# ScalarE's order in the attention with k's high part last, and a normalising stage written out batch by batch, on one core

## The reference

```
x = x + attention(layernorm(x))
x = x + ffn(layernorm(x))            # top 128 of 1024 rows go through gelu(x W1 + b1) W2
attention, for each head h and batch b:
    q, k, v = rope(x Wq), rope(x Wk), x Wv;  g = sigmoid(x Wg)    # three gates for each row and head
    p_cmp = softmax over the means of 64 keys;  p_slc = softmax(q k^T), causal;  p_swa = softmax(q k^T) in a window of 64
    o = g_cmp p_cmp v_cmp + g_slc p_slc v + g_swa p_swa v
out = o Wo
```

## Time and profile before

| | |
|---|---|
| Median of 3 runs | 2583.2 us (2579.54 to 2590.18) |
| The profiled execution | 2591.42 us, its span 2589.3 us |
| Mean granted TensorE clock | 0.978 |
| TensorE busy | 2455.9 us, 95% of the span |
| VectorE / ScalarE / GpSimd busy | 1858.3 / 1412.3 / 1602.1 us |
| Normalising | from 0 to about 100 us of the span |
| Attention | from about 100 to 1970 us |
| Projection with Wo and feed-forward | from 1970 us to the end |

### The profile page before, as it was taken

One profiled execution on the slowest core, in us unless ns is written; L12 is line 12 of the kernel. 1 busy time (PEld: TensorE's weight loads), 2 busy tenths in 40 slices (PEclk: granted clock), 3 DMA queues, 4 the chain that ended last, 5 costly groups with the idle time before them and its releaser, 6 DMA issues. The chain is left out here.

```text
span 2589.3 us, 48591 instructions
## 1 busy us (share of the span) xinstructions
PE 2455.9 (95%) x12944; PEld 2085.2 (81%) x12944; DVE 1858.3 (72%) x5923; ACT 1412.3 (55%) x3810; POOL 1602.1 (62%) x1177
## 2 busy tenths in 40 slices
PE   4799999999999999999999999999996999999998
PEld 3688888888888888888888888888885888887776
DVE  6377878887787878787887878778883576676223
ACT  6466666666666666566666666666663222223342
POOL 0367777777777778677777777777762443443342
PEclk8899999999999999999999999999998999999999
DMA  3222222221212221222222222121215343342266
GB/s 119 65 53 66 59 63 58 64 72 50 69 53 67 54 69 53 69 65 57 64 61 61 61 61 70 52 69 53 61 53 176 120 146 113 130 146 74 89 173 217
DMA packets 145629, 211.74 MB, mean 82 GB/s; under 512 B 14912, under 2 KB 56128, under 8 KB 144576
## 3 DMA queue, kind: packets, MB, share of 16 engines
q1 hardware_dynamic: 145600, 211.37, 27.7%
HBM read 93.87 MB, written 50.33 MB: 56 GB/s over the span
## 5 line engine op out<-in xcount | busy, mean ns | idle before, releaser
L479 PE MATMUL bank<-xt_hi,w_hi 128*128 (+1 forms) x1536 | 630.3, 410 | 45.3 <-ACT vt L563 41.5
L479 PE MATMUL bank<-xt_hi,w_lo 128*128 (+1 forms) x1536 | 608.1, 396 | 0.0
L479 PE MATMUL bank<-xt_lo,w_hi 128*128 (+1 forms) x1536 | 606.2, 395 | 0.0
L440 POOL TENSOR_TENSOR cosed<-s_full,rope 128x512 f32<-128x512 f32 x256 | 329.5, 1290 | 372.5 <-ACT s_full L563 371.0
L479 PEld LDWEIGHTS bank<-xt_hi,w_hi 128*128 128x128 f32 x1536 | 292.9, 191 | 110.4 <-ACT vt L563 48.2
L641 DVE TENSOR_REDUCE shift<-bank 128x1 f32<-128x512 f32 (+3 forms) x512 | 248.4, 485 | 161.7 <-PE bank L508 161.7
L445 POOL TENSOR_TENSOR s_swap<-s_swap,rope 128x512 f32<-128x512 f32 x256 | 329.5, 1287 | 40.6 <-DMA s_swap<-s_full 40.6
L448 POOL TENSOR_TENSOR s_full<-cosed,s_swap 128x512 f32<-128x512 f32 x256 | 331.3, 1294 | 36.7
L479 PEld LDWEIGHTS bank<-xt_hi,w_lo 128*128 128x128 f32 x1536 | 292.9, 191 | 66.6
L479 PEld LDWEIGHTS bank<-xt_lo,w_hi 128*128 128x128 f32 x1536 | 293.8, 191 | 52.8
L452 POOL TENSOR_TENSOR qk_lo<-s_full,qk_hi 128x512 fp32r<-128x512 f32 x256 | 325.3, 1295 | 0.8 <-ACT qk_hi L574 0.8
(11 more groups left out here) (165 smaller groups left out, 5447.6 us busy)
## 6 DMA issues: line engine op xcount, KB each, us to landing
s_swap<-s_full SPq DMA_DIRECT2D x512, 128.0 KB, 2.3
o_scratch<-o_sb SPq DMA_DIRECT2D x128, 256.0 KB, 2.0
o_raw<-o_scratch SPq DMA_DIRECT2D x32, 1024.0 KB, 6.1
xin<-in_L_attn_x SPq DMA_DIRECT2D x16, 1024.0 KB, 5.4
w_raw<-in_L_ffn_W SPq DMA_DIRECT2D x64, 256.0 KB, 3.1
base_scratch<-x SPq DMA_DIRECT2D x8, 1024.0 KB, 4.7
base<-base_scratch SPq DMA_DIRECT2D x32, 256.0 KB, 4.3
out<-base SPq DMA_DIRECT2D x32, 256.0 KB, 3.3
```

The source lines that it names most:

```text
L440: nc.gpsimd.tensor_tensor(cosed[k][:], s_full[k][:], rope[:, 0, :], ALU.mult).then_inc(cos_done[k], 1)
L479: last = nc.tensor.matmul(banks[QB[k]][:, :], w[k][:, c, :], v[:, bass.ds(b, 1), c, :], start=(n == 0), stop=(n == 3 * C - 1))
```

## The change

**In normalise**: everything is written out for 8 batches, with no loop. `xin` has five buffers and is scaled in place, `z` is gone. The first batch is loaded as four tiles with a semaphore each, ahead of `misc`. Small tensors have a place for each batch. VectorE keeps statistics, the reciprocal and `xt_lo`; the refinement goes to GpSimd as six small operations (`refine`). On ScalarE, scaling of batch i+1 comes right behind the high parts of batch i. TensorE transposes batch i+1 ahead of projecting batch i, into six banks in turn. The gates are only copied, and placed by ScalarE in one operation a batch; Sigmoid is applied once to all of them at the start of the attention, where VectorE also applies the factor `some`. The low parts of the first weights go from VectorE to GpSimd.

**In attend**, ScalarE: the copy of output u-3 and `v_hi` of u-2 come behind q's copy (`finish_last`), so a step later than now; then k's copy, the `pt_hi`, row 3; then v's copy, q's high part, rows 2, 1, 0, and k's high part last. The third split of weights stands behind v's copy. SyncE: the store stands between the swaps of q and k, one step later. The low part of the weights is made by VectorE for q (at the start of its body) and v (at its end), and by GpSimd for k.

```diff
-    gates_v = gates[:].rearrange("p (h b) r t -> p h b r t", b=B)
-    xin = r("xin", [P, 2, T, D])
-    z = r("z", [P, T, D])
...
+    gates_v = gates[:].rearrange("p (h b) r t -> p b t r h", b=B)
+    NX, NXB = 5, 6
+    xin = [r(f"xin{s}", [P, T, D]) for s in range(NX)]
...
+    def xbank(i, c):
+        return banks[(i * C + c) % NXB]
...
-            for b in range(B):
-                if b >= 2:
-                    sp.wait_ge(z_ready, T * (b - 1))
-                sp.dma_start(xin[:, b % 2], x[b].rearrange("(t p) d -> p t d", p=P)).then_inc(x_loaded[b % 2], 16)
-                if b == 0:
-                    sp.dma_start(misc[:], misc_d).then_inc(misc_loaded, 16)
+            for t in range(T):
+                sp.dma_start(xin[0][:, t], x[0, t * P:(t + 1) * P, :]).then_inc(first_loaded[t], 16)
+            sp.dma_start(misc[:], misc_d).then_inc(misc_loaded, 16)
+            for b in range(1, B):
+                if b >= NX:
+                    sp.wait_ge(xt_transposed, (b - NX + 1) * C)
+                sp.dma_start(xin[b % NX][:], x[b].rearrange("(t p) d -> p t d", p=P)).then_inc(x_loaded[b % NX], 16)
+                if b == 1:
                     sp.wait_ge(wg_zeroed, 1)
                     sp.dma_start(wg_raw[:, :, 0:3 * H], wg.rearrange("(c p) n -> p c n", p=P)).then_inc(wg_loaded, 16)
             weights.load(sp, 0)
...
+                pool.wait_ge(inverted, i + 1)
+                g.tensor_tensor(yy[:, i], y[:, i], y[:, i], ALU.mult).then_inc(newton, 1)
+                pool.wait_ge(newton, i * NN + 1)
...
+                g.tensor_scalar(minus[:, i], y[:, i], -1.0, None, ALU.mult).then_inc(newton, 1)
+                pool.wait_ge(newton, i * NN + 5)
+                g.tensor_tensor(minus[:, i], minus[:, i], mv[:, i, :, 0], ALU.mult).then_inc(newton, 1)
...
+            g.memset(wg_raw[:], 0.0).then_inc(wg_zeroed, 1)
+            refine(0)
+            refine(1)
             pool.wait_ge(wg_split, 1)
-            nc.gpsimd.tensor_tensor(wg_lo[:], wg_raw[:], f32(wg_hi[:]), ALU.subtract).then_inc(wg_split, 1)
+            g.tensor_tensor(wg_lo[:], wg_raw[:], f32(wg_hi[:]), ALU.subtract).then_inc(wg_split, 1)
+            for i in range(2, B):
+                refine(i)
+            for k in range(3):
+                weights.low(pool, g, 0, k)
...
-            dve.wait_ge(misc_loaded, 16)
-            steps(dve, body)
-            for k in range(3):
-                weights.low(dve, nc.vector, 0, k)
...
+            def measure(i):
+                for t in range(T):
+                    if i == 0:
+                        dve.wait_ge(first_loaded[t], 16)
+                    elif t == 0:
+                        dve.wait_ge(x_loaded[i % NX], 16 * ((i - 1) // NX + 1 if i % NX else i // NX))
+                    v.bn_stats(stats[:, i, t], xin[i % NX][:, t]).then_inc(stats_done, 1)
+                for t in range(T):
+                    dve.wait_ge(stats_done, i * 2 * T + T)
+                    v.bn_aggr(mv[:, i, t], stats[:, i, t]).then_inc(stats_done, 1)
+                dve.wait_ge(stats_done, i * 2 * T + 2 * T)
+                v.tensor_scalar(ve[:, i], mv[:, i, :, 1], EPS, None, ALU.add).then_inc(ve_ready, 1)
+            def invert(i):
+                dve.wait_ge(sd_ready, i + 1)
+                v.reciprocal(y[:, i], sd[:, i]).then_inc(inverted, 1)
+            def low(i):
+                for c in range(C):
+                    dve.wait_ge(xt_hi_ready, i * C + c + 1)
+                    v.tensor_tensor(xt_lo[:, i, c, :], xbank(i, c)[:, :], f32(xt_hi[:, i, c, :]), ALU.subtract).then_inc(xt_lo_ready, 1)
+            measure(0)
+            invert(0)
+            measure(1)
+            invert(1)
+            measure(2)
+            for i in range(B):
+                if i + 2 < B:
+                    invert(i + 2)
+                low(i)
+                if i + 3 < B:
+                    measure(i + 3)
...
+            def root(i):
+                act.wait_ge(ve_ready, i + 1)
+                nc.scalar.activation(sd[:, i], ve[:, i], ACT.Sqrt).then_inc(sd_ready, 1)
+            def scale(i):
+                act.wait_ge(newton, i * NN + NN)
+                for t in range(T):
+                    nc.scalar.activation(xin[i % NX][:, t], xin[i % NX][:, t], ACT.Identity, bias=minus[:, i, t:t + 1],
+                                         scale=y[:, i, t:t + 1]).then_inc(z_ready, 1)
+            def high(i):
+                for c in range(C):
+                    act.wait_ge(xt_transposed, i * C + c + 1)
+                    nc.scalar.activation(xt_hi[:, i, c, :], xbank(i, c)[:, :], ACT.Copy).then_inc(xt_hi_ready, 1)
+            def copy_gates(i):
+                act.wait_ge(g_projected, i + 1)
+                if i >= 2:
+                    act.wait_ge(g_turned, i - 1)
+                nc.scalar.activation(ge[i % 2][:], banks[6][:, :], ACT.Copy).then_inc(g_copied, 1)
+            def place_gates(i):
+                act.wait_ge(g_turned, i + 1)
+                nc.scalar.activation(gates_v[:, i], banks[7][:, :].rearrange("p (t q) -> p t q", t=T)[:, :, 0:3 * H]
+                                     .rearrange("p t (r h) -> p t r h", r=3), ACT.Copy).then_inc(g_placed, 1)
+            root(0)
+            scale(0)
+            root(1)
+            act.wait_ge(wg_loaded, 16)
+            nc.scalar.activation(wg_hi[:], wg_raw[:], ACT.Copy).then_inc(wg_split, 1)
+            for i in range(B):
+                if i + 2 < B:
+                    root(i + 2)
+                high(i)
+                if i + 1 < B:
+                    scale(i + 1)
+                if i >= 2:
+                    place_gates(i - 2)
+                if i >= 1:
+                    copy_gates(i - 1)
             for k in range(3):
                 weights.high(act, 0, k)
+            place_gates(B - 2)
+            copy_gates(B - 1)
+            place_gates(B - 1)
...
+            def turn(i):
+                pe.wait_ge(z_ready, i * T + T)
+                for c in range(C):
+                    if i * C + c >= NXB:
+                        pe.wait_ge(xt_lo_ready, i * C + c - NXB + 1)
                     for t in range(T):
...
+                        last = nc.tensor.transpose(xbank(i, c)[:, t * P:(t + 1) * P], xin[i % NX][:, t, c * P:(c + 1) * P], m("ident"))
+                    last.then_inc(xt_transposed, 1)
+            def project(i):
+                pe.wait_ge(xt_lo_ready, i * C + C)
+                if i:
+                    pe.wait_ge(g_copied, i)
...
+            def turn_gates(i):
+                pe.wait_ge(g_copied, i + 1)
+                if i:
+                    pe.wait_ge(g_placed, i)
+                for t in range(T):
+                    last = nc.tensor.transpose(banks[7][:, t * P:(t + 1) * P], ge[i % 2][:, t * P:(t + 1) * P], m("ident"))
+                last.then_inc(g_turned, 1)
             pe.wait_ge(misc_loaded, 16)
-            pe.wait_ge(wg_split, 2)
-            steps(pe, body)
+            turn(0)
+            for i in range(B):
+                if i + 1 < B:
+                    turn(i + 1)
+                if i == 0:
+                    pe.wait_ge(wg_split, 2)
+                if i >= 1:
+                    turn_gates(i - 1)
+                project(i)
+            turn_gates(B - 1)
...
-            def body(u, b, project, score, end):
+            def store(u):
+                sp.wait_ge(out_evacuated, u - 1)
+                sp.dma_start(o_dram[bass.ds(u - 3, 1)].rearrange("o p n -> p (o n)"), o_sb[:]).then_inc(out_slot_free, 16)
+            def body(u, project, output):
                 if project:
                     swap(u, 0)
+                if output:
+                    store(u)
+                if project:
                     swap(u, 1)
-                if end:
-                    sp.wait_ge(out_evacuated, u)
-                    sp.dma_start(o_dram[bass.ds(u - 2, 1)].rearrange("o p n -> p (o n)"), o_sb[:]).then_inc(out_slot_free, 16)
...
             def body(u, b, project, score, end, split):
                 if project:
-                    for k in range(2):
-                        turn_cos(u, k)
-                        if split is not False:
-                            weights.low(pool, nc.gpsimd, split, k)
+                    turn_cos(u, 0)
+                    turn_cos(u, 1)
+                    if split is not False:
+                        weights.low(pool, nc.gpsimd, split, 1)
                     for part in (turn_sin, low):
                         for k in range(2):
                             part(u, k)
-                    if split is not False:
-                        weights.low(pool, nc.gpsimd, split, 2)
...
-            def body(u, b, project, score, end, split):
-                for k in range(2):
-                    if project:
-                        evacuate(u, k)
-                    if split is not False:
-                        split_weights(split, k)
+            def finish_last(u, values, output):
+                if output:
```

(71 more changed lines are left out.)

155 lines of the change are left out of this document (39 added, 116 removed).

## The result

The changed kernel takes **2,504.1 us** (median of 4 runs, 2,502.2 to 2,506.8), the kernel before 2,586.7 in the runs beside it: ratio 0.9685, 95% interval 0.9658 to 0.9711, so 82.6 us faster. The forecast was 2,496 with a range of 2,480 to 2,522. The profiled executions span 2,589.3 and 2,502.3 us.

| part | before, us | after, us | gained | forecast |
|---|---|---|---|---|
| normalising, to the first projection | 100.7 | 71.0 | 29.7 | 27 |
| start of the attention | 43.5 | 34.4 | 9.1 | 6 |
| heads | 1,788.6 | 1,741.3 | 47.2 | 54 |
| end of the attention and all behind it | 656.6 | 655.6 | 1.0 | 4 |

The account below looks back on a forecast made before the run. Attention was taken as bound by TensorE (busy 98%), normalising by a chain of waits. Gains 54 + 6 + 4 + 27 = 91 us off the profiled 2,591.4 gave 2,500, or 2,492 by median; forecast 2,496, range 2,480 to 2,522.

Parts of the forecast that it names:

- Normalising, 27 us: Normalising stage: batches decoupled at 6.7 us each, one table load left, end at 73 against 100 us; bounds 12 and 30.
- Rival 2: Normalising stays a chain, by TensorE's lower clock or slow GpSimd small operations: gains 12 us instead of 27, 2,511; chance 0.17.
- Start of the attention, 6 us: First 48 us of attention: v's early copy removes TensorE's two waits for `vt`, plus some clock; 6 us, bounds 2 and 8.
- Heads, 54 us: Changes of head: 59.2 us lost today, less about 5 still lost; regular step stays at 13.83 us.
- (e): Split step, low parts on VectorE: 0.3 us lost, 15 times; a GpSimd contention rule spoke against it, left out of sum.
- rival 1: Head changes not healed, stall moves to another link or VectorE's split: 2 us a head remain, 2,521; chance 0.12.
- (b): ScalarE's row 3 ahead of q, k's high part last: `sums` at S+15.7, v's low part covered by 0.45 us, price nothing.
- Rival 3: Slower than before: k's or v's low part late every step, needing 1.2 us beyond the cover; 2,621 at 1.0; chance 0.04.
- (c): Last output's stores and copies and `v_hi` moved to the next step, behind q's copy: costs nothing.
- (d): SyncE issues weight loads right after k's swap; with v's copy moved, the load's 14 x 3.2 = 45 us gained in full.
- (a): ScalarE copies v ahead of q's high part, at S+12.2: slack grows from 0.6 to over 3.5 us, removing the load's stall.
- End, 4 us: End of attention: Wo's first chunk issued earlier, v's high part making transposes about 1 us later; 4 us, bounds 0 and 6.

Follow-up runs that it names:

- before_v_early: Kernel before, with one ScalarE edit: v's copy right behind row 3's exponentials, still behind q's high part; 2,582.1 us, ratio 0.9988.
- attention_alone: Changed attention with the old normalising stage of the kernel before, Sigmoid staying in that stage; 2,534.0 us, ratio 0.9803 against the kernel before.
- normalise_alone: Changed normalising stage with the old attention of the kernel before, Sigmoid ahead of that attention; 2,554.3 us, ratio 0.9881 against the kernel before.

## Why the prediction was right, point by point

- **Normalising, 27 us: 29.7.** The chain is gone as described. A batch takes 6.2 us (starts of the four scalings of a batch at 32.20, 38.44, 44.68 and 50.92) instead of 6.7, a little under the 6.4 that I had as the least. Of the 13 table loads of 1.28 one is left in the stage, at 0.74; that of the Sigmoid is at 70.97, where the attention starts. Two errors meet in the total: the eighth scaling starts at 56.5 and not at 61.8, but from there to the first projection it takes 14.5 us and not 11. The groups of 0 to 71 us, beside the earlier trace rows:

```profile
L262 ACT ACTIVATE xin<-xin,minus,y 128x512 f32<-128x512 f32 x32 | 23.4, 818 | 2.0 <-POOL minus L202 2.0
L239 DVE TENSOR_TENSOR xt_lo<-bank,xt_hi 128x512 fp32r<-128x512 f32 x32 | 20.1, 683 | 8.4 <-ACT xt_hi L268 8.4
...
L200 POOL TENSOR_SCALAR minus<-y 128x4 f32<-128x4 f32 x8 | 1.8, 221 | 0.7
```

  The work of ScalarE and VectorE is unchanged, only its idle time fell. GpSimd's small operations take 0.19 to 0.22 us, not the 0.3 that I took or the 1.29 of the bound. Rival 2 did not come true: the stage ends at 71 us, with a clock of 0.95.
- **Start of the attention, 6 us: 9.1.** Both waits for `vt` went, and what is left in 71 to 120 us is 0.8 us each for `qk_lo` and `s_full` and 2.3 in five waits for the probabilities. v's early copy is the main cause: 5.1 us on its own in before_v_early, of 6.5 for the whole new order in attention_alone. The rest, 2.4, comes with the new normalising stage (normalise_alone). The granted clock over this stretch is 0.84 before, 0.92 in either half alone and 1.00 after; the forecast had it as "some clock" and gave it no size.
- **Heads, 54 us: 47.2.** The regular step stayed at 13.83 and the load's 45 us went in full. The term that was mis-sized is **(e), the split step: 0.3 us taken, 0.8 measured** (12.0 / 15). Two parts: 6.6 of the 12.0 us, 0.4 a head, from the third high part ahead of `sums`, where I allowed 0.1 to 0.2 since I counted on cover that wasn't there, and 5.4 from VectorE's low parts beside GpSimd, of which 0.42 in each of nine heads. The trace agrees with the rule that spoke against (e): where VectorE's low parts have two inputs in SBUF, at least one of the two engines runs longer each time, by up to 1.1 us. The Trainium skill (GPSIMD Engine Reference, Specifications) names this pairing. I had it only stop GpSimd, inside cover, as it did in six heads; what cost time was VectorE's own half, 0.68 become 1.80, with v's projection waiting for it. That is a part of rival 1, at 0.5 us a head rather than 2.
- **(b), cover of 0.45 us: none.** The step stays at 13.83 all the same, so the sum was right, but by luck: half a microsecond more would have been paid in every step. The failed step is the list of consumers: the scores that overwrite the probabilities' banks were not in it. Rival 3 (each step late) was thus nearer than the 0.04 and the "1.2 us beyond the 0.45 of cover" say: with k's high part where it had been, some 62 of the change's 82.6 us are gone.
- **(c)** nothing, as said. **(d)** right and sufficient: the loads alone give the whole 45, so that (a) was not needed for them, against the forecast's "with (a)". (a) earns its keep at the start. One reading of the earlier trace rows was wrong in a detail: behind the wait of 2.09 us TensorE restarts at the upper clock, its products 0.23 us apart until 824.36, and only then falls to the lower, 0.43 apart until 827.31.
- **End, 4 us: 1.0.** The delay of v's high part was mis-sized (1 us taken, 3.6 measured), and what `wo_lo` and `o_lo` cost each other was not in the sum at all.
- **Sum, 91 us: 87.0.** Heads and end gave 9.8 us less than forecast, start and normalising 5.8 more, so part of the closeness is errors that cancel. The other part of the 8 us between 2,496 and 2,504 is the base. The forecast is 87.2 under the median of before that I had, 2,583.2; in the runs beside the changed kernel, and in the three groups, that median was 2,585.8 to 2,588.3. Against 2,586.7 the change gained 82.6: 4.6 of the 8 us are the gain, 3.5 the base.

## What to carry to other kernels

When an order on one engine is changed, list for the step every wait that its results release, the ones for a free bank too, and count cover against the earliest; where the earliest has no cover left, a half microsecond moved in a queue is paid in every step. A transfer that is issued by the engine that also issues the urgent ones is worth moving first: three transfers issued about ten microseconds earlier gave 48 us by themselves, where all the edits to the attention together gave 53. An operation that has two inputs in SBUF belongs on VectorE only where GpSimd is idle or where nobody is near to wait for it.

## What the runs showed of the hardware

- VectorE and GpSimd hold each other up when VectorE subtracts two SBUF tiles, and the one that finds the other running pays: 512 columns on VectorE took 0.68 us where both began together, with GpSimd's at up to 1.83 instead of 1.29, and up to 1.81 where GpSimd was first and kept its 1.27; 2,048 columns took 2.29 with GpSimd idle and 5.13 behind GpSimd's 4.52. I had expected GpSimd alone to pay. Beside VectorE's reads of PSUM GpSimd kept its 1.29.
- TensorE's granted clock fell behind a wait of some 2 us in nine of 14 heads and stayed at 1.00 in five; where it fell, the step behind took 1.6 us more (14.94 instead of 13.34).
- A queue with no cover passes a delay on in full, not in part: ScalarE's 0.52 us became 0.55 in some 115 steps.
- GpSimd's operations on four columns cost 0.19 to 0.22 us, no more than ScalarE's root of the same four columns (205 ns), though its 512 columns take 1.29 where VectorE's take 0.68.
